# Recommender kernel: three placements moved in the last layers of the previous chunk (first transposes, second layer with its bias, Gelu)

## The chip, the cores and the metric

The kernel runs on one core of a Trainium2 chip. The metric is the device time in microseconds (us). TensorE (PE in the profile), VectorE (DVE), ScalarE (ACT), GpSimd (POOL) and the DMA queue of SyncE (SP) each work through their own instructions in order and meet at semaphores.

## The reference

2048 rows, each with 5 fields of 128 numbers (one of them attention over 50 history items), are expanded to 15 features of 128 (`TOTAL_DIM` = 1920). Then come two cross layers and a network of three layers:

```python
xc = dnn_in
for i in range(2):
    xc = dnn_in * (xc @ cross_K[i] + cross_bias[i]) + xc
h = gelu(_ln(xc @ w1 + b1, ln1g, ln1b), approximate=False)   # 1920 -> 512
h = gelu(_ln(h @ w2 + b2, ln2g, ln2b), approximate=False)    # 512 -> 256
logits = h @ w3 + b3
return sigmoid(logits)[:, 0]
```

The attention of one row scores each history item with a small network (`relu(x @ aw1 + ab1) @ aw2 + ab2`), takes the softmax and sums the items with these weights.

## The kernel before

The 16 tiles of 128 rows are cut into four chunks of four tiles (`T` = 4). After an opening, which does the attention of chunk 0, each chunk runs 30 steps `k` = 0 to 29 (15 output features of the first cross layer, then 15 of the second) and then the layer with `w1`. A step is three blocks of 15 matmuls on TensorE (`products(..., 0)`, `1`, `2`), each a third of the sum over the input features. Between the blocks TensorE's queue holds small work of two other kinds, put there by hand:

- The attention of the next chunk's tiles. `transposes(t, g, 0)` goes behind block 0 and `transposes(t, g, 1)` behind block 1, both for groups of ten history items; they write the PSUM tile `aps`, which a ScalarE copy (`copy_eT(0)`, `copy_eT(1)`) frees through `tp_free`. `hidden()` goes behind block 0 of the step after, `score()` behind its block 2. VectorE answers with `hidden_max`; in the step after that it does `softmax_max`, ScalarE does `exps` and `weigh`, and VectorE does `history` (a sum over the weighed items). `head_aim` stands on VectorE at the end of step 3 and of every sixth step after. Chunk 3 has no such work, because there is no chunk behind it.
- The last layers of the chunk ahead (`T and ...` in the code, in chunks 1 to 3 alone), at steps 2 to 9. For tile j: `fc_turn1(j)` transposes the normed `h1` of the tile into the fourth bank of `xps` (`FCB`); `fc_gelu1(j)` on ScalarE takes it out and frees the bank; `fc_w2(j)` multiplies by `w2` into the same bank; `fc_bias2(j)` on VectorE takes that out and frees the bank. `bank4_free` hands the bank round, so the order is turn1(j), gelu1(j), w2(j), bias2(j), turn1(j+1). `head_share` and `head_neg` of the attention use the same bank at steps 6 and 7. When all four tiles are through, `fc_stats`, `fc_sd` (a square root on ScalarE) and `fc_norms2` follow at step 6, `fc_turn2` at steps 7 and 8, `fc_w3` at step 9.

On ScalarE and VectorE each step also holds three `unit`s: `w_hi` rounds a weight block to the short form (`Wh`), `w_lo` subtracts it (`Wl`), for a block three ahead of the one at TensorE. Every `w_lo` waits for its `w_hi`. The order on VectorE in step k is: `x_sum`, `softmax_max`, first `w_lo`, `x_scale`, `fc_bias2`, `x_end`, `hidden_max`, `history`, second `w_lo`, `x_lo`, `times_target`, third `w_lo`, `head_aim` and `fc_stats`. On ScalarE it is: first `w_hi`, `exps` and `weigh`, `x_hi`, `copy_eT(0)`, second `w_hi`, `fc_gelu1`, `copy_eT(1)`, `fc_gelu2`, third `w_hi`, `fc_sd`.

Of the kernel before, what the change touches and what calls it, by code (L numbers as in the profile page):

```python
# [140 lines left out]
def build(nc, idx_d, table_d, cate_d, embT_d, rows_d, cols_d, mmw_d, aw1_d, bil_d, kx_d, w1_d, w2_d, out_d, ntiles):  # L141
    assert sum(TILES) == ntiles
    with ExitStack() as ctx:
# [92 lines left out]
        def h2(j):  # L236

            return h1[:, j, 0:H2]
# [91 lines left out]
        fvar_ready = sem("fvar_ready")  # L330
# [121 lines left out]
        def _(pe):  # L452
# [26 lines left out]
            def head_turn():  # L479
                pe.wait_ge(tgt_ready, 1).then_inc(tgt_ready, -1)  # L480
                pe.wait_ge(tp_free, 1).then_inc(tp_free, -1)
                nc.tensor.transpose(gps, tgt[:], ident[:]).then_inc(tp_ready, 1)
# [116 lines left out]
            def fc_turn1(j, bank=FCB):  # L599
                pe.wait_ge(h1n_ready, 1).then_inc(h1n_ready, -1)  # L600
                if bank == FCB:
                    pe.wait_ge(bank4_free, 1).then_inc(bank4_free, -1)
                for k in range(H1 // P):
                    last = nc.tensor.transpose(xps[:, bank, k * P:(k + 1) * P], h1[:, j, k * P:(k + 1) * P], ident[:])
                last.then_inc(fT_ready, 1)

            def fc_w2(j, bank=FCB):
                pe.wait_ge(g_ready, 1).then_inc(g_ready, -1)
                if bank == FCB:
                    pe.wait_ge(bank4_free, 1).then_inc(bank4_free, -1)  # L610
                for k in range(H1 // P):
                    last = mm(xps[:, bank, 0:H2], h1_T(j)[:, k, :], w2[:, k, :], start=(k == 0), stop=(k == H1 // P - 1))
                last.then_inc(fmm_ready, 1)
# [40 lines left out]
            def step(p):  # L654
                T, k = p.fc, p.k
                products(p.chunk, p.layer, p.n, 0)
                if T and 2 <= k < T + 2:
                    fc_turn1(k - 2)
                if p.open:
                    hidden()  # L660
                if p.pair is not None:
                    tail_bilinear()
                if p.grp:
                    transposes(*p.grp, 0)

                products(p.chunk, p.layer, p.n, 1)
                if p.grp:
                    transposes(*p.grp, 1)
                elif p.swing is not None:
                    head_turn()  # L670
                if T and k == T + 3:
                    fc_turn2(pairs(T)[0])
                if T > 2 and k == T + 4:
                    fc_turn2(pairs(T)[1])
                if T and k == T + 5:
                    fc_w3(T)

                products(p.chunk, p.layer, p.n, 2)
                if T and 2 <= k < T + 2:
                    fc_w2(k - 2)  # L680
                if p.share is not None:
                    head_share(p.share)
                if p.open:
                    score()
                if p.lift is not None:
                    tail_turn(p.lift)
# [13 lines left out]
            T = TILES[-1]  # L700
# [11 lines left out]
        def _(act):  # L712
# [36 lines left out]
            def copy_tT(t):  # L749
                act.wait_ge(tp_ready, 1).then_inc(tp_ready, -1)  # L750
                done(af(tT[:, t % 2, :], gps, ACT.Copy))
                act.sem_inc(tp_free, 1)
                act.sem_inc(tT_ready, 1)
# [81 lines left out]
            def fc_gelu1(j, bank=FCB):  # L835
                act.wait_ge(fT_ready, 1).then_inc(fT_ready, -1)
                for k in range(H1 // P):
                    last = af(h1_T(j)[:, k, :], xps[:, bank, k * P:(k + 1) * P], ACT.Gelu, scale=col("g1", k), bias=col("lb1", k))
                done(last)
                if bank == FCB:  # L840
                    act.sem_inc(bank4_free, 1)
                act.sem_inc(g_ready, 1)
# [55 lines left out]
            def step(p):  # L898
                c, k, T = p.chunk, p.k, p.fc

                if c and k == 0:
                    r_hi(c, FEATS - 1)
                if T and k == T + 6:
                    fc_exp(c - 1)
                if T and k == T + 7:
                    fc_out(c - 1)
                if p.pair is not None:
                    tail_copy(p.pair)
                unit(c, 3 * k)
                if p.fetch is not None:  # L910
                    head_fetch(p.fetch)
                if p.summed:
                    exps(*p.summed)
                    weigh(*p.summed)
                if p.n or p.layer:
                    x_hi(*((c, p.layer, p.n - 1) if p.n else (c, 0, FEATS - 1)))
                if p.gate is not None:
                    tail_gate()

                if p.grp:  # L920
                    copy_eT(0)
                unit(c, 3 * k + 1)
                if T and 2 <= k < T + 2:
                    fc_gelu1(k - 2)

                if p.grp:
                    copy_eT(1)
                elif p.swing is not None:
                    copy_tT(p.swing)
                if T and k == T + 3:  # L930
                    fc_gelu2(pairs(T)[0])
                if T > 2 and k == T + 4:
                    fc_gelu2(pairs(T)[1])
                unit(c, 3 * k + 2)
                if p.pair is not None:
                    tail_store(p.pair)
                if T and k in (1, T + 2):
                    fc_sd(T)
# [44 lines left out]
        def _(dve):  # L983
# [211 lines left out]
            def unit_out(c, b):  # L1195
                if c * STREAM + b + LOOK < TOTAL:
                    w_out()


            def fc_stats(j, x):  # L1200
                done(v.bn_stats(fstats[:], x))
                done(v.bn_aggr(fmv[:, j, :], fstats[:]))
# [13 lines left out]
            def fc_bias2(j, bank=FCB):  # L1216
                dve.wait_ge(fmm_ready, 1).then_inc(fmm_ready, -1)
                done(v.tensor_tensor(h2(j), xps[:, bank, 0:H2], row("b2"), ALU.add))
                if bank == FCB:
                    dve.sem_inc(bank4_free, 1)  # L1220
# [49 lines left out]
            def step(p):  # L1270
                c, k, T = p.chunk, p.k, p.fc
                prev = (c, p.layer, p.n - 1) if p.n else (c, 0, FEATS - 1) if p.layer else None

                if c and k == 0:
                    r_lo(c, FEATS - 1)
                if prev:
                    x_sum(*prev)
                if p.summed:
                    softmax_max(*p.summed)
                if T and k == 0:  # L1280
                    h1_rest(c - 1)
                unit(c, 3 * k)
                if prev:
                    x_scale(*prev)
                unit_out(c, 3 * k)
                if T and 3 <= k < T + 3:
                    fc_bias2(k - 3)
                if p.neg is not None:
                    head_neg(p.neg)
                if prev:  # L1290
                    x_end(*prev)
                if T and k == T + 2:
                    fc_stats(T - 1, h2(T - 1))
                    dve.sem_inc(fvar_ready, 1)
                if p.open:
                    hidden_max(p.open[0])
                if p.summed:
                    history(*p.summed)

                unit(c, 3 * k + 1)  # L1300
                if prev:
                    x_lo(*prev)
                unit_out(c, 3 * k + 1)
                if p.pair is not None:
                    tail_pairs()
                if p.grp:
                    times_target(p.grp[0])

                unit(c, 3 * k + 2)
                unit_out(c, 3 * k + 2)  # L1310
                if T and k == T + 6:
                    fc_probs(c - 1)
                if p.gate is not None:
                    tail_gate_apply(p.gate)
                if p.fold is not None:
                    tail_fold(p.fold)
                if p.aim is not None:
                    head_aim(p.aim)
                if T and k == 0:
                    for j in range(T):  # L1320
                        fc_stats(j, h1[:, j, :])
                    dve.sem_inc(fvar_ready, 1)
                if T and k == 1:
                    fc_norms1(T)
                if T and 3 <= k < T + 2:
                    fc_stats(k - 3, h2(k - 3))
                if T and k == T + 2:
                    fc_norms2(T)
# [115 lines left out]
```

## Time and profile before

| what | value |
|---|---|
| median of 3 runs | 2120.38 us (2118.11 to 2121.18) |
| span of the profiled execution | 2115.6 us |
| TensorE busy | 1937.3 us, 92% |
| VectorE busy | 1337.0 us, 63% |
| ScalarE busy | 904.3 us, 43% |
| mean granted TensorE clock | 0.941 |

The page cuts the span into 40 slices of 52.9 us. From the eighth on TensorE is busy for over nine tenths of each until near the end; the opening is the part where it is not. The timeline lists instructions in order of time; an idle stretch of the engine before an instruction stands behind it in brackets, with the line that ended it (`PEq L602` is the wait of TensorE's own queue on line 602).

### The profile page before, as it was taken

To read this page: it belongs to the slowest core of one execution; us is meant where nothing else is said; L and a number is where in the kernel's file an instruction comes from. 1 tells how busy PE (TensorE), PEld (TensorE's weight loads), DVE (VectorE), ACT (ScalarE), POOL (GpSimd) and SP (SyncE) were. 2 spreads that over 40 slices of the span, in tenths; PEclk is the share of its full clock that TensorE was granted. 3 is DMA by queue.
4 is the path that set the end of the run, shared out by engine and by line. 5 is a ranking of instruction groups with operands and counts; after the bars stand their busy time and mean duration, and the time that the engine had idled before them with its cause. 6 is when DMAs were issued, how large, how long until landed. Compare 5 with 4: busy or idle time off the path is not lost. (4 is left out here: it accounts for less than half of the span.)

```text
span 2115.6 us, 32889 instructions
## 1 busy us (share of the span) xinstructions
PE 1937.3 (92%) x9608; PEld 1518.8 (72%) x9608; DVE 1337.0 (63%) x2242; ACT 904.3 (43%) x1969; POOL 894.1 (42%) x854
## 2 busy tenths in 40 slices
PE   1765659999999999999999999999999999999997
PEld 1444437777777887777777886777777888888885
DVE  4564564767777755667777755666777664445543
ACT  1443443444444335654445235654445243322223
POOL 7777776555655512555555601555560000000000
PEclk7666568999999999999999999999999999999998
DMA  5111123334434452334434452334432442333330
GB/s 164 50 51 50 49 51 102 104 102 129 120 109 122 143 190 68 100 95 127 118 111 123 148 175 63 100 111 115 120 107 90 129 158 81 89 99 96 97 91 15
DMA packets 99679, 220.31 MB, mean 104 GB/s; under 512 B 21792, under 2 KB 27184, under 8 KB 99376
## 3 DMA queue, kind: packets, MB, share of 16 engines
q1 hardware_dynamic: 63072, 136.90, 21.5%
q0 software_dynamic: 27136, 55.63, 10.4%
q10 hardware_dynamic: 9296, 25.70, 3.2%
q8 instruction: 80, 1.31, 0.3%
q14 instruction: 95, 0.78, 0.1%
HBM read 205.29 MB, written 12.85 MB: 103 GB/s over the span
## 5 line engine op out<-in xcount | busy, mean ns | idle before, releaser
L415 POOL DMA_INDIRECT e<-in_item_table,idx_all x800 | 842.9, 1054 | 651.9 <-issue 303.8
L1148 DVE TENSOR_TENSOR Wl<-raw,Wh 128x640 fp32r<-128x640 f32 (+1 forms) x420 | 338.2, 805 | 286.6 <-DVEq L1147 283.0
L808 ACT ACTIVATE Wh<-raw 128x640 fp32r<-128x640 f32 (+1 forms) x420 | 301.8, 722 | 494.7 <-ACTq L807 493.7
L550 PE MATMUL xps<-X0h,Wh 128*128 128x512 f32 x900 | 364.7, 405 | 0.0
L550 PE MATMUL xps<-X1h,Wh 128*128 128x512 f32 x900 | 359.4, 399 | 0.0
L552 PE MATMUL xps<-X0h,Wl 128*128 128x512 f32 x900 | 352.1, 391 | 0.0
L551 PE MATMUL xps<-X0l,Wh 128*128 128x512 f32 x900 | 351.7, 391 | 0.0
L552 PE MATMUL xps<-X1h,Wl 128*128 128x512 f32 x900 | 351.0, 390 | 0.0
L551 PE MATMUL xps<-X1l,Wh 128*128 128x512 f32 x900 | 350.7, 390 | 0.0
L767 ACT ACTIVATE e<-e,pw 128x128 f32<-128x128 f32 x800 | 242.8, 388 | 15.4 <-ACTq L138 15.4
L552 PEld LDWEIGHTS xps<-X0h,Wl 128*128 128x128 f32 x900 | 169.4, 188 | 37.2
L552 PEld LDWEIGHTS xps<-X1h,Wl 128*128 128x128 f32 x900 | 168.9, 188 | 36.5
L550 PEld LDWEIGHTS xps<-X0h,Wh 128*128 128x128 f32 x900 | 169.8, 189 | 34.1 <-issue 2.1
L550 PEld LDWEIGHTS xps<-X1h,Wh 128*128 128x128 f32 x900 | 169.2, 188 | 33.6 <-issue 1.0
L551 PEld LDWEIGHTS xps<-X0l,Wh 128*128 128x128 f32 x900 | 170.1, 189 | 31.2
L551 PEld LDWEIGHTS xps<-X1l,Wh 128*128 128x128 f32 x900 | 169.4, 188 | 32.2
L1087 DVE TENSOR_REDUCE hist<-e 128x128 f32<-128x1280 f32 (+1 forms) x65 | 156.0, 2399 | 49.3 <-DVEq L1085 49.3
L736 ACT ACTIVATE eT<-aps 128x640 f32<-128x640 f32 x141 | 98.1, 696 | 166.6 <-ACTq L735 166.1
L1039 DVE TENSOR_TENSOR teT<-eT,tT 128x1280 f32<-128x1280 f32 x79 | 117.7, 1490 | 64.3 <-DVEq L1037 64.3
L492 PE MATMUL hps<-eT,A 128*64 128x512 f32 (+2 forms) x640 | 137.4, 509 | 19.7 <-PEq L486 19.6
L467 PE MATMUL aps<-ident,e 128*128 128x128 f32 x700 | 109.7, 290 | 37.9 <-issue 27.5
L496 PE MATMUL hps<-teT,A 128*64 128x512 f32 (+2 forms) x640 | 134.4, 499 | 0.0
(149 smaller groups left out, 2181.4 us busy)
## 6 DMA issues: line engine op xcount, KB each, us to landing
raw<-in_cross_K SPq DMA_DIRECT2D x360, 320.0 KB
raw<-in_w SPq DMA_DIRECT2D x60, 256.0 KB
e<-in_item_table,idx_all POOLq DMA_INDIRECT x800, 2.5
dnn_scratch<-dn ACTq DMA_DIRECT2D x12, 960.0 KB, 4.2
x1f<-dnn_scratch ACTq DMA_DIRECT2D x3, 2048.0 KB, 9.3
x1f<-dnn_scratch ACTq DMA_DIRECT2D x3, 1792.0 KB, 15.0
dn<-in_embT SPq DMA_DIRECT2D x1, 1024.0 KB, 5.3
img_scratch<-dn ACTq DMA_DIRECT2D x1, 1024.0 KB, 4.6
```

Of the source, the lines that this page charges most:

```text
L415: nc.gpsimd.indirect_dma_start(out=dst, out_offset=None, in_=table, in_offset=bass.IndirectOffsetOnAxis(ap=idx_all[:, t, s:s + 1], axis=0) ...
L467: last = nc.tensor.transpose(tps[:, s * P:(s + 1) * P], e_sub(t, g, u, s), ident[:])
L492: last = mm(hsum[u * HID:(u + 1) * HID, a:b], A12[:], eT[:, u, a:b], start=True, stop=False)
L496: last = mm(hsum[u * HID:(u + 1) * HID, a:b], A3[:], teT[:, u, a:b], start=False, stop=True)
L550: m0 = mm(out, wh, Xh[:, 0:T, k, :], start=(k == 0), stop=False)
L551: m1 = mm(out, wh, Xl[:, 0:T, k, :], start=False, stop=False)
L552: m2 = mm(out, wl, Xh[:, 0:T, k, :], start=False, stop=(k == FEATS - 1))
L767: last = af(x, x, ACT.Copy, scale=pw[:, g % 2, s:s + 1])
L808: af(Wh[:, split_slot(w), 0:n], raw[:, rs, 0:n], ACT.Copy).then_inc(hi_done, 1)
L1039: v.tensor_tensor(teT[:].rearrange("p u (s b) -> p (u s) b", b=P), eT[:].rearrange("p u (s b) -> p (u s) b", b=P), tT[:, par:par + 1, :].t ...
L1087: done(v.tensor_reduce(hist[:] if g else acc[:, par, :], x, AX.X, ALU.add))
L1148: v.tensor_tensor(Wl[:, rs, 0:n], raw[:, rs, 0:n], Wh[:, slot, 0:n].bitcast(F32), ALU.subtract).then_inc(lo_done, 1)
```

## The change

TensorE: `fc_turn1(k - 2)` moves from behind block 0 to behind block 1 and the second transposes of step k. `fc_w2` moves from behind block 2 of step k to behind block 0 of step k + 1. ScalarE: `fc_gelu1(k - 2)` moves from before to behind `copy_eT(1)`, still in step k and still before the third `w_hi`. VectorE: `fc_bias2(k - 3)`, and at step 6 the statistics of the last tile, move from behind the first `w_lo` to behind the second `w_lo` and `x_lo` of the same step. No instruction is added or taken away.

```diff
@@ tensor, step(p)
                 products(p.chunk, p.layer, p.n, 0)
-                if T and 2 <= k < T + 2:
-                    fc_turn1(k - 2)
+                if T and 3 <= k < T + 3:
+                    fc_w2(k - 3)
                 if p.open:
                     hidden()
...
                     head_turn()
+                if T and 2 <= k < T + 2:
+                    fc_turn1(k - 2)
                 if T and k == T + 3:
                     fc_turn2(pairs(T)[0])
...
                 products(p.chunk, p.layer, p.n, 2)
-                if T and 2 <= k < T + 2:
-                    fc_w2(k - 2)
@@ scalar, step(p)
                 unit(c, 3 * k + 1)
-                if T and 2 <= k < T + 2:
-                    fc_gelu1(k - 2)
-
                 if p.grp:
                     copy_eT(1)
                 elif p.swing is not None:
                     copy_tT(p.swing)
+                if T and 2 <= k < T + 2:
+                    fc_gelu1(k - 2)
@@ vector, step(p)
                 unit_out(c, 3 * k)
-                if T and 3 <= k < T + 3:
-                    fc_bias2(k - 3)
...
-                if T and k == T + 2:
-                    fc_stats(T - 1, h2(T - 1))
-                    dve.sem_inc(fvar_ready, 1)
...
                 unit_out(c, 3 * k + 1)
+                if T and 3 <= k < T + 3:
+                    fc_bias2(k - 3)
+                if T and k == T + 2:
+                    fc_stats(T - 1, h2(T - 1))
+                    dve.sem_inc(fvar_ready, 1)
```

## Rows read from the trace of the kernel before

**Rows 1.** The page: busy time of each engine, share of the span.

```profile
PE 1937.3 (92%) x9608; PEld 1518.8 (72%) x9608; DVE 1337.0 (63%) x2242; ACT 904.3 (43%) x1969; POOL 894.1 (42%) x854
```

**Rows 2.** Waits of TensorE: line <- released by: us in total, times, longest.

```profile
PE xps L604 <- PEq L602: 6.5, 2, 3.5
```

**Rows 3.** Timeline, TensorE, chunk 1: start, us, line, what, [idle before].

```profile
825.25 0.76 PE L467 MATMUL aps<-ident,e 128*128 128x128 f32 x5
829.27 0.71 PE L467 MATMUL aps<-ident,e 128*128 128x128 f32 x5
...
842.72 0.63 PE L604 MATMUL xps<-ident,dn 128*128 128x128 f32 x4 [3.04 <-PEq L602]
...
860.01 0.63 PE L604 MATMUL xps<-ident,dn 128*128 128x128 f32 x4
...
897.60 0.74 PE L467 MATMUL aps<-ident,e 128*128 128x128 f32 x5 [1.84 <-PEq L465]
```

**Rows 4.** Timeline, VectorE, chunk 1, from the end of step 3 to step 4.

```profile
825.48 0.82 DVE L1053 TENSOR_TENSOR hidT<-hps,negT 128x640 f32<-128x640 f32 x1 [3.39 <-DVEq L1052]
...
833.76 0.82 DVE L1148 TENSOR_TENSOR Wl<-raw,Wh 128x640 fp32r<-128x640 f32 x1
...
842.01 0.42 DVE L1218 TENSOR_TENSOR dn<-xps,rows 128x256 f32<-128x256 f32 x1
845.81 0.82 DVE L1053 TENSOR_TENSOR hidT<-hps,negT 128x640 f32<-128x640 f32 x1 [3.39 <-DVEq L1052]
...
847.02 2.46 DVE L1087 TENSOR_REDUCE hist<-e 128x128 f32<-128x1280 f32 x1 [0.26 <-DVEq L1085]
...
851.08 0.69 DVE L1189 TENSOR_TENSOR X1l<-x1f,X1h 128x512 fp32r<-128x512 f32 x1
...
854.09 0.82 DVE L1148 TENSOR_TENSOR Wl<-raw,Wh 128x640 fp32r<-128x640 f32 x1
```

**Rows 5.** Timeline, ScalarE, chunk 1, steps 3 to 5.

```profile
828.10 1.28 ACT L838 ACT_TABLE_LOAD   x1
...
831.32 0.71 ACT L736 ACTIVATE eT<-aps 128x640 f32<-128x640 f32 x1 [0.42 <-ACTq L735]
...
840.78 1.28 ACT L759 ACT_TABLE_LOAD   x1 [3.42 <-ACTq L757]
...
858.08 1.28 ACT L759 ACT_TABLE_LOAD   x1 [0.38 <-ACTq L757]
```

**Rows 6.** Timeline, VectorE, chunk 1, steps 6 and 7.

```profile
877.54 0.43 DVE L1201 BATCH_NORM_STATS2 tiny<-dn 128x6 f32<-128x256 f32 x1 [0.54 <-DVEq L1176]
...
886.81 0.18 DVE L1206 RECIPROCAL frstd<-fsd 128x4 f32<-128x4 f32 x1 [0.35 <-DVEq L1205]
...
896.38 2.37 DVE L1087 TENSOR_REDUCE hist<-e 128x128 f32<-128x1280 f32 x1 [2.12 <-DVEq L1085]
```

**Rows 7.** Timeline, ScalarE, chunk 1, steps 6 and 7.

```profile
884.92 1.28 ACT L833 ACT_TABLE_LOAD   x1
...
891.13 1.28 ACT L759 ACT_TABLE_LOAD   x1 [1.71 <-ACTq L757]
```

**Rows 8.** Timeline, TensorE, ScalarE and VectorE, chunk 3.

```profile
1811.83 0.60 PE L622 MATMUL xps<-ident,dn 128*128 128x128 f32 x4
...
1812.54 1.28 ACT L848 ACT_TABLE_LOAD   x1 [2.09 <-ACTq L845]
...
1765.06 0.74 ACT L808 ACTIVATE Wh<-raw 128x640 fp32r<-128x640 f32 x1 [1.29 <-ACTq L807]
...
1765.94 0.82 DVE L1148 TENSOR_TENSOR Wl<-raw,Wh 128x640 fp32r<-128x640 f32 x1 [2.00 <-DVEq L1147]
```

**Rows 9.** Timeline, chunk 2: TensorE at step 4, then VectorE's answer.

```profile
1315.54 1.09 PE L604 MATMUL xps<-ident,dn 128*128 128x128 f32 x4 [3.50 <-PEq L602]
...
1320.16 0.82 DVE L1053 TENSOR_TENSOR hidT<-hps,negT 128x640 f32<-128x640 f32 x1 [4.92 <-DVEq L1052]
```

**Rows 10.** Busy time by stretch (PE, PEld, DVE, ACT, POOL, PEclk, DMA share, GB/s).

```profile
1315.50:1319.00 3.50, 3.46 (x12) 1.52 (x14) 0.00 (x0) 3.35 (x11) 1.03 (x2) 0.54 0.13 37
```

## The prediction
> **What bounds the kernel now.** I read the page's busy times first: TensorE is busy 92% of the span, VectorE 63%, and the slices put most of TensorE's idle time into the opening [rows 1]. So from chunk 0 on an edit is worth what it adds to or takes from TensorE's idle time. Next come TensorE's waits: the only one in the chunks that names the moved code is line 602, the first transposes waiting for `bank4_free`, twice, 6.5 us in all, the longest 3.5 [rows 2]. Then the timelines, to see where. In chunk 1 the wait is 3.04 us at step 4 [rows 3], in chunk 2 it is 3.50 us at the same step [rows 9], and chunk 3 has none. The reader is to see why it is step 4: `fc_bias2`, which frees the bank, starts at 842.01 on VectorE, 0.71 us before the transposes at 842.72 [rows 3, 4]; it was late because `head_aim` lies between the third `w_lo` of step 3 (833.76) and the `softmax_max` that lets ScalarE's exponential begin (840.78), 7.02 us, where a step without `head_aim` takes 858.08 - 854.09 = 3.99 us [rows 4, 5]. At step 7 TensorE waits 1.84 us for `aps` (line 465), behind another chain [rows 3].
>
> **What the change removes.** The transposes no longer stand behind block 0, where `fc_bias2` was late. That gives back at most 3.04 + 3.50 us. In chunk 2 the wait also cost clock: the granted clock is 0.54 in the 3.50 us behind it [rows 10], that is, mostly the lower level (1.2 GHz), and from the transposes' start to `hidden_max` it is 4.62 us (1320.16 - 1315.54), against 845.81 - 842.72 = 3.09 us in chunk 1 [rows 3, 4, 9]: 1.53 us more. About 0.3 us of small waits at steps 3 and 5 may go too. The gain is at most 8.4 us. No instruction is added, and each moved piece still stands beside other small work, so I put nothing on TensorE's own work.
>
> **What the change adds: VectorE's side of the bank.** From step 3 on, the transposes of a tile wait for `fc_bias2` of the tile before, which now stands behind `hidden_max`, `history`, the second `w_lo` and `x_lo` of the same step. I count from the start of `hidden_max`, H, which comes as TensorE ends `hidden`. `x_lo` starts at H + 5.27 (851.08 - 845.81) [rows 4], `fc_bias2` about 0.6 later (the length of `x_lo`, 0.69, less its overlap), and the transposes 0.71 after its start: H + 6.6. TensorE reaches them after the second transposes of the attention: those start at 829.27, 3.79 after H (825.48), and last about 0.5, so at H + 4.25 [rows 3, 4]. The new wait is 2.35 us at steps 4 and 5. At step 3 `history` handles a first group and has no accumulation behind it, some 0.6 less: 1.75 us. What queues behind the waiting transposes is block 2, so all of TensorE.
>
> **What the change adds: a loop through three engines.** `fc_gelu1` on ScalarE now waits for transposes that are late in the step, and behind it in ScalarE's queue stands the third `w_hi`; VectorE's third `w_lo` waits for that, and behind `w_lo` stand `head_aim` and the next step's `softmax_max`. S is the start of the transposes.
> - S to ScalarE's table load for Gelu: 0.71 (1812.54 - 1811.83, a like pair in chunk 3) [rows 8].
> - Table load, Gelu and the link behind it, to the next instruction: 831.32 - 828.10 = 3.22 [rows 5]. So the third `w_hi` starts at S + 3.93.
> - `w_hi` to `w_lo`: 0.88 (1765.94 - 1765.06) [rows 8]. S + 4.81.
> - `w_lo` to the exponential's table load: 3.99, with `head_aim` 7.02 (above).
> - From there to `history`, which needs the weighed items: 896.38 - 891.13 = 5.25 [rows 6, 7].
> - `history` to `x_lo` 4.06 (851.08 - 847.02), to `fc_bias2` 0.6, to the next transposes 0.71: 5.37 [rows 3, 4].
>
> The sum is 4.81 + 3.99 + 5.25 + 5.37 = 19.4 us per step, and 22.45 us from step 3 to step 4 with `head_aim`. Step 4 to step 5 took 860.01 - 842.72 = 17.29 us before [rows 3]. So the loop is longer than TensorE's step, and each step runs at the loop's time. TensorE is then the waiter, though its work is the same.
>
> **The sum for chunk 1**, as the start of block 2 of each step (before: H + 4.25; after: S + 0.35, since the four transposes add that to the ones beside them):
> - Step 3: H was 825.48; without the transposes ahead of it 0.65 less, 824.8. S = 824.8 + 6.0 = 830.8, block 2 at 831.2 against 829.7: 1.4 us late.
> - Step 4: S = 830.8 + 22.45 = 853.3, block 2 at 853.6 against 850.06: 3.6 us late (gaps of about 5.5 us in place of 3.04; part of them before the second transposes, since `copy_eT(0)`, which frees `aps`, is behind `weigh`).
> - Step 5: S = 853.3 + 19.4 = 872.7, block 2 at 873.1 against 845.81 + 17.29 + 4.25 = 867.35: 5.7 us late.
> - Steps 6 and 7: the exponential's load is at 872.7 + 4.81 + 3.99 = 881.5, `history` at 886.8, `fc_bias2` 4.66 later at 891.4, and with the last tile's statistics (which took 0.43 and a little more [rows 6]) ScalarE's square root loads at about 892.9. It was at 884.92 [rows 7], so 8.0 us late. What hangs on it is as before: reciprocal 1.89 later, then 4.32 to the exponential's load at 891.13, then 6.47 to the second transposes at 897.60 [rows 3, 6, 7]. They come at about 905.6: 8.0 us late, in place of a wait of 1.84 some 4.3.
>
> `head_share` at step 6 needs the bank as well: `fc_bias2` at 891.4 frees it by 892.1, and TensorE is there at about 892.1, so nothing is added. Behind step 7 the same waits follow as before. **Chunk 2** is the same with 0.46 us more of old wait and 1.53 us of old clock loss in its time: 8.0 - 2.0 = 6.0 us. **Chunk 3** has no `history`, no exponential and no late `x_lo`: the transposes come a whole block later and so does the bank; 0, at most 0.5 us. Sum without the clock: 14.0 us.
>
> **The clock.** A gap of 3.50 us was followed by a low clock [rows 9, 10], and one of 3.04 us was not: there `hidden_max` follows the transposes at the ordinary 3.09 us [rows 3, 4]. The new gaps of about 5.5 us at step 4 (in two pieces) and 4.3 us at step 7, in both chunks, are four such places. One lapse cost 1.53 us [rows 9], at step 4 nearly all of it added because the path by H is 19.2 us, close to the loop. I take two of the four, 3.0 us, with 0 and 6.1 as the bounds. The Trainium skill ("TensorE: Matmul & The Clock Gate", Part 1: The HAM clock gate) says that an idle array falls back to half rate and only activity releases it, which speaks against this change; the chunk 2 gap agrees, at 0.54. By that rule all four places would lapse, and the time would be 2140.5 us.
>
> **The rivals.**
> - The gain that the moved lines offer: TensorE finds the bank free in all steps. 2120.4 - 8.4 = 2112.0 us. For it: the transposes come a block and more later in the step. Against: `fc_bias2` moves by more, 851.7 against 842.01 at step 4 (9.7 us), and the transposes by about 7.3 (from 839.68, where the wait began, to 850.06 less the 3.04 us of wait). It decides if `history` were short; it is 2.46 us [rows 4].
> - VectorE's delay alone, without the loop (if `w_hi` did not have to wait for Gelu): each step takes the path by H, 19.2 us, step 4 too, and block 2 is late by 1.4, 0.3 and 2.2 us; the square root then follows `fc_bias2` of step 6 and step 7 is 4.2 us late. Chunk 1 +4.2, chunk 2 +2.2: 2126.8 us. Against: `unit(c, 3 * k + 2)` stands behind `fc_gelu1` in ScalarE's queue.
> - All four lapses and waits carried into steps 8 and 9: 14.0 + 6.1 + 2 to 6 us, 2143 to 2147 us. For it: step 7 already waits before the change [rows 3], so a lapse in its block 2 could meet the next copy late. Against: VectorE and ScalarE are held by the same TensorE and come later with it.
> - No difference that shows: the new waits equal the old in size. It needs new waits of 5 us a chunk; the least that I find is the second rival's.
>
> **How the numbers follow.** The profiled span, 2115.6 us, is 4.8 us under the median, which I take as constant. Forecast: 14.0 + 3.0 = 17.0 us, a span of 2132.6, a median of 2137.4 us. Chances: the forecast (2131 to 2141) 0.56; VectorE's delay alone (2124.6 to 2131) 0.15; all lapses 0.12; no difference 0.08; the gain 0.09. About 0.2% (4.2 us) is what a measurement of this kernel tells from no change. Slower by more: 0.83; within: 0.08; faster: 0.09. The range leaves out the gain, no difference and the top of the third rival: 2124 to 2145 us.
>
> **What would show it.** In the profile after: line 602 as TensorE's largest wait of the chunks, at steps 3, 4 and 5 of chunks 1 and 2 with about 1.8, 3.4 and 2.4 us; a wait on line 465 at step 4 of about 2 us and at step 7 of about 4; the third `w_hi` right behind Gelu and the third `w_lo` 0.9 us behind that; chunk 3 unchanged. I am wrong on the loop if step 4 to step 5 takes under 19 us from transposes to transposes, and wrong on the direction if line 602 no longer appears.

## The result, and the profile after

| | before | after |
|---|---|---|
| median | 2120.41 us (2118.11 to 2121.18) | 2140.45 us (2139.80 to 2141.72) |
| span of the profiled execution | 2115.6 us | 2138.9 us |
| TensorE busy | 1937.3 us | 1941.0 us |
| mean granted TensorE clock | 0.941 | 0.937 |

The ratio of after to before is 1.0089, with a 95% interval of 1.0077 to 1.0101: the changed kernel is 20.0 us slower by the medians, 23.3 us by the two profiled spans. I had forecast 17.0 us. The first two figures differ because the profiled execution of before was a quick one: in the changed kernel a run's time is 1.8 us over its span, and so I estimate that before's profiled execution took 2117.4 us, 3.0 under its median. Where those 3 us lie is open, since before has one profile only.

First TensorE's waits in the changed kernel (line <- released by: us in total, times, longest), to be held against [rows 2]. `L467` is the attention's transposes waiting for `aps`, `L604` the first transposes of the last layers waiting for the bank.

```profile
PE aps L467 <- PEq L465: 17.4, 11, 3.9
PE xps L604 <- PEq L602: 13.8, 6, 3.3
```

The reader is to see the count: two bank waits have become six. The timeline of TensorE in chunk 1 shows where; the number in brackets is the wait.

```profile
831.60 0.63 PE L604 MATMUL xps<-ident,dn 128*128 128x128 f32 x4 [1.52 <-PEq L602]
...
849.94 0.74 PE L467 MATMUL aps<-ident,e 128*128 128x128 f32 x5 [1.58 <-PEq L465]
853.99 1.08 PE L604 MATMUL xps<-ident,dn 128*128 128x128 f32 x4 [3.31 <-PEq L602]
...
875.40 1.09 PE L604 MATMUL xps<-ident,dn 128*128 128x128 f32 x4 [2.08 <-PEq L602]
...
909.71 1.30 PE L467 MATMUL aps<-ident,e 128*128 128x128 f32 x5 [3.89 <-PEq L465]
```

These are steps 3, 4, 4, 5 and 7; chunk 2 has the same five (1.51, 1.80, 3.31, 2.08 and 3.91 us), chunk 3 none. Where [rows 3] had 0.63 us for four transposes and 0.74 us for five, three of these groups are drawn out (1.08, 1.09 and 1.30 us): the clock is low there, as the windows further down show.

One stretch serves from here on as the measure of every kernel: from the second attention transposes of step 1 to those of step 9, in chunks 1 and 2. The columns are length, then busy time of PE, PEld, DVE, ACT and POOL, granted clock, DMA share, GB/s. The kernel before:

```profile
797.70:929.40 131.70, 125.10 (x663) 96.69 (x664) 82.72 (x143) 81.17 (x161) 57.53 (x53) 1.00 0.31 88
1270.05:1403.40 133.35, 126.54 (x664) 97.27 (x664) 82.70 (x143) 81.16 (x161) 55.49 (x53) 0.99 0.31 87
```

The changed kernel:

```profile
798.40:942.30 143.90, 130.39 (x664) 100.86 (x665) 82.86 (x143) 80.92 (x161) 55.75 (x53) 0.95 0.28 80
1282.80:1427.20 144.40, 130.33 (x663) 100.85 (x664) 83.01 (x143) 80.91 (x161) 55.03 (x53) 0.95 0.28 80
```

The two stretches have grown by 12.2 and 11.05 us, together 23.25 us, which is the whole difference of the spans (3 us more than that of the medians). Length less TensorE's busy time is its idle time: 6.6 + 6.8 us before, 13.5 + 14.1 us after, so 14.2 us are new waits. The other 9.1 us are busy time: the same matmuls (664, one record more or less) took 125.10 and 126.54 us, and now 130.39 and 130.33 us. VectorE and ScalarE worked as long as before.

The low clock by stretch: the end of the wait of step 4, then the time after the waits of step 4, step 5 and step 7 of chunk 1. The clock is the column before the DMA share:

```profile
850.00:854.00 4.00, 0.69 (x6) 0.48 (x6) 3.19 (x5) 1.44 (x2) 1.64 (x2) 0.68 0.00 0
854.00:858.00 4.00, 4.00 (x12) 3.32 (x13) 1.49 (x1) 2.79 (x5) 3.09 (x4) 0.50 0.32 70
875.40:879.00 3.60, 3.60 (x11) 3.04 (x12) 1.49 (x1) 2.39 (x5) 2.99 (x3) 0.53 0.21 44
909.70:913.20 3.50, 3.50 (x14) 3.16 (x15) 3.00 (x5) 2.42 (x3) 1.13 (x2) 0.54 0.08 19
```

The last three are nearly all at the lower level (1.2 GHz). At step 4 the clock has fallen before the wait is over (0.68), and stays low for 4 us of work more. The loop through the three engines can be read off between step 3 and step 4 (ScalarE, VectorE; VectorE's line numbers are one lower than before):

```profile
832.34 1.28 ACT L838 ACT_TABLE_LOAD   x1 [1.34 <-ACTq L836]
...
835.55 0.74 ACT L808 ACTIVATE Wh<-raw 128x640 fp32r<-128x640 f32 x1 [0.42 <-ACTq L807]
...
843.48 1.28 ACT L759 ACT_TABLE_LOAD   x1 [5.61 <-ACTq L757]
```

```profile
836.44 0.83 DVE L1147 TENSOR_TENSOR Wl<-raw,Wh 128x640 fp32r<-128x640 f32 x1 [3.29 <-DVEq L1146]
...
848.72 2.35 DVE L1086 TENSOR_REDUCE hist<-e 128x128 f32<-128x1280 f32 x1 [2.53 <-DVEq L1084]
...
853.27 0.42 DVE L1217 TENSOR_TENSOR dn<-xps,rows 128x256 f32<-128x256 f32 x1
```

From the transposes at 831.60: Gelu's table load 0.74 later, third `w_hi` at + 3.95, third `w_lo` at + 4.84 after 3.29 us of waiting for it, the exponential's load 7.04 behind that with `head_aim` between, `history` 5.24 later after 2.53 us of waiting for `weigh`, `fc_bias2` 4.55 later, the next transposes 0.72 later at 853.99.

### The profile page after: what moved, and what is told of

Same layout as the page of the kernel before. It is cut to its first block and busy times, and to the rows that moved or that the text cites. A ratio compares the mean times of both kernels' runs of the same rounds, so it can differ in the third digit from the quotient of the medians.

```text
span 2138.9 us, 32889 instructions
## 1 busy us (share of the span) xinstructions
PE 1941.0 (91%) x9608; PEld 1522.7 (71%) x9608; DVE 1336.4 (62%) x2242; ACT 903.6 (42%) x1969; POOL 891.4 (42%) x854
## 5 line engine op out<-in xcount | busy, mean ns | idle before, releaser
L467 PE MATMUL aps<-ident,e 128*128 128x128 f32 x700 | 110.6, 292 | 46.4 <-issue 29.0
L467 PEld LDWEIGHTS aps<-ident,e 128*128 128x128 f32 x700 | 85.1, 149 | 71.3 <-issue 63.5
```

The lines of the kernel that those rows point to most:

```text
L467: last = nc.tensor.transpose(tps[:, s * P:(s + 1) * P], e_sub(t, g, u, s), ident[:])
```

## The experiments

In the table, "waits" is TensorE's idle time in the two stretches, "busy" its busy time there. The rows e1 to e9 are the experiments in the order of the sections below.

| kernel | median, us | ratio to before (95%) | stretches, us | waits, us | busy, us |
|---|---|---|---|---|---|
| before | 2120.4 | | 265.05 | 13.4 | 251.6 |
| after | 2140.5 | 1.0089 (1.0077 to 1.0101) | 288.3 | 27.6 | 260.7 |
| e1_bias_early | 2120.5 | 0.9994 (0.9985 to 1.0003) | 267.6 | 12.1 | 255.5 |
| e2_gelu_late | 2134.5 | 1.0062 (1.0048 to 1.0076) | 281.7 | 22.1 | 259.6 |
| e3_both | 2109.1 | 0.9944 (0.9930 to 0.9957) | 255.3 | 6.3 | 249.0 |
| e4_aim_moved | 2133.4 | 1.0055 (1.0042 to 1.0069) | 266.6 | 12.4 | 254.2 |
| e5_filled | 2134.1 | 1.0059 (1.0045 to 1.0073) | 279.3 | 7.6 | 271.7 (46 matmuls more in each) |
| e6_bias_first | 2122.4 | 1.0005 (0.9996 to 1.0014) | 267.7 | 13.9 | 253.8 |
| e7_after_again | 2139.5 | one run | 288.2 | 27.7 | 260.5 |
| e8_norms_late | 2107.2 | 0.9938 (0.9924 to 0.9951) | 253.2 | 4.1 | 249.1 |
| e9_both_again | 2109.0 | 0.9944 (0.9931 to 0.9958) | 255.6 | 6.4 | 249.2 |

The kernel before had medians of 2120.5 to 2121.5 us beside these. Of the stretches each row is one profile. Two kernels were profiled twice, and their stretches agree to 0.1 us (288.3 and 288.2) and 0.3 us (255.3 and 255.6). Ahead of chunk 1 all but e4 run the same code, yet they reach the first row of the stretch anywhere from 796.9 to 802.4 us: single spans differ by that without any cause in the change.

### VectorE's move undone

```diff
                 unit_out(c, 3 * k)
+                if T and 3 <= k < T + 3:
+                    fc_bias2(k - 3)
                 if p.neg is not None:
                     head_neg(p.neg)
                 if prev:
                     x_end(*prev)
+                if T and k == T + 2:
+                    fc_stats(T - 1, h2(T - 1))
+                    dve.sem_inc(fvar_ready, 1)
...
                 unit_out(c, 3 * k + 1)
-                if T and 3 <= k < T + 3:
-                    fc_bias2(k - 3)
-                if T and k == T + 2:
-                    fc_stats(T - 1, h2(T - 1))
-                    dve.sem_inc(fvar_ready, 1)
```

> The changed kernel with fc_bias2 and the last tile's statistics put back behind VectorE's first w_lo. My theory: VectorE then waits there for fc_w2, which ends over 2 us before hidden, so hidden_max is not late; the bank is free when TensorE comes to the transposes, line 602 disappears from its waits, and the loop through Gelu, softmax_max and history no longer has a way back to the transposes. What stays is a wait of 1.5 to 2 us on aps (line 465) at step 4 and the old 1.84 us at step 7. Against before: - 3.04 - 3.50 - 1.53 - 0.3 + 2 x 1.9 = -4.6 us, 2115.8 us. Rival: ScalarE's order (Gelu ahead of the third w_hi) costs the time by itself; then it stays over 2130 us with waits on aps at each step.

Measured: 2120.53 us, the time of the kernel before. TensorE has no wait on the bank left in chunks 1 and 2; what is left at steps 4 and 7 of chunk 1 are waits for `aps`:

```profile
852.91 0.96 PE L467 MATMUL aps<-ident,e 128*128 128x128 f32 x5 [2.26 <-PEq L465]
...
903.34 0.74 PE L467 MATMUL aps<-ident,e 128*128 128x128 f32 x5 [2.37 <-PEq L465]
```

The theory is right on the bank and the rival is out: 20.7 of the stretches' 23.25 us go with this one edit. The gain that I expected on top did not come, for two reasons. The wait at step 4 is 2.26 us, not 1.9, and step 7's grew from 1.84 to 2.37 us; and behind these waits the clock is low (0.55 and 0.67 in the 3.5 us that follow, chunk 1), so that busy time is 3.9 us above that of before.

### Gelu behind the third `w_hi`

```diff
                 elif p.swing is not None:
                     copy_tT(p.swing)
-                if T and 2 <= k < T + 2:
-                    fc_gelu1(k - 2)
...
                 unit(c, 3 * k + 2)
+                if T and 2 <= k < T + 2:
+                    fc_gelu1(k - 2)
```

> The changed kernel with fc_gelu1 put behind ScalarE's third w_hi; everything else of the change stays. My theory: VectorE's third w_lo no longer waits for Gelu, so only the path hidden_max, history, w_lo, x_lo, fc_bias2 is left: waits on line 602 of about 1.8, 2.4 and 2.4 us at steps 3, 4 and 5, step 4 no longer the longest, chunk 1 +4.2 us and chunk 2 +2.2 us, 2126.8 us, up to 2131 where the clock lapses. Rival: the late fc_bias2 is the whole cause and the loop adds nothing; then it stays at 2138 us or more.

Measured: 2134.51 us. TensorE in chunk 1, steps 3, 4, 5 and 7:

```profile
831.59 0.63 PE L604 MATMUL xps<-ident,dn 128*128 128x128 f32 x4 [1.50 <-PEq L602]
...
851.12 0.63 PE L604 MATMUL xps<-ident,dn 128*128 128x128 f32 x4 [2.23 <-PEq L602]
...
872.12 0.63 PE L604 MATMUL xps<-ident,dn 128*128 128x128 f32 x4 [2.08 <-PEq L602]
...
906.43 0.74 PE L467 MATMUL aps<-ident,e 128*128 128x128 f32 x5 [3.89 <-PEq L465]
```

The waits on the bank are the ones that the path through `hidden_max` and `history` gives, and step 4 is no longer apart: 2.23 us in place of 1.58 + 3.31. From step 3 to step 4 it is 19.53 us between the transposes (851.12 - 831.59), where the changed kernel has 22.39. So the loop is real, and it is worth 5.5 us of waiting in the two stretches (27.6 - 22.1). But the time is 3.5 us above the top of what I expected, since the clock falls behind three waits of each chunk here too (in chunk 1 0.70, 0.63 and 0.60 in the 3.5 us from each of the last three rows); the busy time is 8 us above that of before.

### Both edits

The edits of the two kernels above together; TensorE's new order stays.

```diff
@@ scalar, step(p)
-                if T and 2 <= k < T + 2:
-                    fc_gelu1(k - 2)
...
                 unit(c, 3 * k + 2)
+                if T and 2 <= k < T + 2:
+                    fc_gelu1(k - 2)
@@ vector, step(p)
                 unit_out(c, 3 * k)
+                if T and 3 <= k < T + 3:
+                    fc_bias2(k - 3)
...
+                if T and k == T + 2:
+                    fc_stats(T - 1, h2(T - 1))
+                    dve.sem_inc(fvar_ready, 1)
...
                 unit_out(c, 3 * k + 1)
-                if T and 3 <= k < T + 3:
-                    fc_bias2(k - 3)
-                if T and k == T + 2:
-                    fc_stats(T - 1, h2(T - 1))
-                    dve.sem_inc(fvar_ready, 1)
```

> The changed kernel with both edits: fc_bias2 behind VectorE's first w_lo, fc_gelu1 behind ScalarE's third w_hi. TensorE's new order stays. My theory: no wait on line 602, at most 0.7 us on aps at step 4, step 7 as before: 2112 to 2114 us, faster than before. Rival: TensorE's new order itself costs (more changes between kinds of matmul, later tiles at steps 6 and 7); then it is at 2120 us or above.

Measured: 2109.07 us, 12.3 us under before, and 2108.95 us when run again (below), 11.6 under. The two stretches:

```profile
797.00:924.80 127.80, 124.58 (x663) 96.59 (x664) 82.58 (x143) 81.13 (x161) 58.11 (x53) 1.00 0.31 90
1265.40:1392.90 127.50, 124.44 (x663) 96.56 (x664) 82.51 (x143) 81.13 (x161) 57.12 (x53) 1.00 0.30 91
```

The granted clock is 1.00 in both, and no wait stands at step 4 at all. The wait at step 7 is 1.61 us. So TensorE's new order costs nothing that shows, once the other two engines' queues fit it, and the rival is out. This kernel and the one with VectorE's move undone differ in the place of Gelu alone, and that is worth 12.3 us of the stretches (267.6 - 255.3). How much of the gain over before belongs to TensorE's order and how much to Gelu's place is not shown: no run has the old order with Gelu moved. It beat the expected 2112 us by 3 us. Step 7's wait fell a little too, and the busy time of chunk 1 is 124.58 us where before had 125.10, both at a clock of 1.00; that the transposes now run beside others of their kind may be why, but no run tests it.

### `head_aim` moved, in the kernel before

```diff
-            fetch, aim, swing = s - 6, s - 4, s - 1
+            fetch, aim, swing = s - 6, s - 2, s - 1
```

> The kernel before with head_aim of the tiles of later chunks two steps later (at step 5 and every sixth after, in place of step 3): no transposes wait for the bank at step 6. My theory: head_aim is what made fc_bias2 late at step 4, so line 602 disappears from the waits, worth 3.04 + 3.50 + 1.53 us; but softmax_max of step 6 is then about 3.0 us late, history 2.7 us, and the wait on aps at step 7 grows from 1.84 to about 4.5 us. Sum 5.3 - 8.1 = -2.8 us, 2117.6 us, or 2120.6 us where the clock lapses at step 7. Rival: something else makes fc_bias2 late at step 4 (ScalarE's w_hi, the score); then the wait on line 602 stays at 3 us and the time is 2123 us or more.

Measured: 2133.43 us, a miss by 13 us. In the part that it was made for it did what I said: chunk 1 has no wait on the bank, chunk 2 one of 0.66 us, and the wait at step 7 has taken its place, with a low clock behind it (0.50 in 3.5 us). TensorE, steps 1 and 7 of chunk 1:

```profile
810.93 0.74 PE L467 MATMUL aps<-ident,e 128*128 128x128 f32 x5 [1.02 <-PEq L465]
...
910.63 1.30 PE L467 MATMUL aps<-ident,e 128*128 128x128 f32 x5 [4.73 <-PEq L465]
```

The stretches are 1.6 us longer than before. The larger part of the loss, 13.2 us, is there when chunk 1 begins (810.93 against 797.74), 8.5 us later than in the latest of the other kernels: the edit also moved `head_aim` of the other tiles of chunks 1 to 3, in the opening and in chunk 0. What it did there was not taken apart.

### TensorE kept at work in the waits of the changed kernel

```diff
+            FILL = {3: (0, 6), 4: (6, 12), 5: (0, 8), 7: (14, 0)}
+            def fill(p, at):
+                ...
+                for i in range(FILL[p.k][at]):
+                    mm(out, Wh[:, split_slot(w), 0:P], X0h[:, 0:TILES[c], 0, :], start=True, stop=True)
...
                 products(p.chunk, p.layer, p.n, 1)
+                fill(p, 0)
                 if p.grp:
                     transposes(*p.grp, 1)
                 elif p.swing is not None:
                     head_turn()
+                fill(p, 1)
```

TensorE's wait for the next output feature's bank (`bank_free`) moves ahead of these matmuls with them.

> The changed kernel with extra matmuls on TensorE (fp32r, 512 columns, 0.23 us apart, into the bank of the next output feature, which is not yet in use) in front of the waits of chunks 1 and 2: 6 ahead of the first transposes at step 3, 6 ahead of the second attention transposes and 12 ahead of the first transposes at step 4, 8 at step 5, 14 ahead of the second attention transposes at step 7. They are work for nothing, 46 matmuls or 10.5 us a chunk, shorter than each wait that they stand in. My theory: some 9.5 us of the change's cost is the low clock behind the waits; with TensorE kept at work it stays high, and the time falls from 2140 to about 2131 us (2129 to 2133), with no stretch of low clock in chunks 1 and 2. Rival: the time is in the waits alone and the low clock is absorbed by them; then the filled kernel stays at 2140 us or goes above, since it has more work.

Measured: 2134.11 us, 1.1 us above the expected range and 6.3 us faster than the changed kernel (5.4 against its run beside this one), with 92 matmuls more.

```profile
799.80:939.50 139.70, 135.92 (x710) 104.81 (x711) 83.03 (x143) 80.70 (x161) 56.44 (x53) 1.00 0.29 83
1280.10:1419.70 139.60, 135.77 (x710) 104.88 (x710) 82.95 (x143) 80.69 (x161) 55.73 (x53) 1.00 0.29 83
```

The clock column says 1.00. The stretches are 9.0 us shorter than those of the changed kernel (279.3 against 288.3), close to the 9.1 us that its busy time had gained over before. So that some 9 us of the loss come with the low clock is shown, not only read, and the rival is out. The match is in part chance: before has 1.5 us of low clock in its own stretches, so the changed kernel has about 10.6 (an estimate: 260.7 less twice the 125.1 of before's chunk 1), and the filled kernel is some 15.8 us over a kernel before without it. Removing 10.6 us of low clock gave 9.0 us, and the waits took up the rest. The median fell by less than the stretches. From transposes to transposes, steps 4 and 5, at the high clock:

```profile
855.50 0.63 PE L617 MATMUL xps<-ident,dn 128*128 128x128 f32 x4 [0.59 <-PEq L615]
...
874.96 0.63 PE L617 MATMUL xps<-ident,dn 128*128 128x128 f32 x4 [0.31 <-PEq L615]
```

19.46 us, against the 19.4 us of the prediction's sum. This figure doesn't tell the loop from the path through `hidden_max`, which took 19.53 us without the loop (above): from step 4 to step 5 the two are equally long. What shows the loop is step 3 to step 4, where `head_aim` lies in it.

### `fc_bias2` ahead of `softmax_max`, in the kernel before

```diff
                 if prev:
                     x_sum(*prev)
+                if T and 3 <= k < T + 3:
+                    fc_bias2(k - 3)
                 if p.summed:
                     softmax_max(*p.summed)
...
-                if T and 3 <= k < T + 3:
-                    fc_bias2(k - 3)
```

> The kernel before with fc_bias2 put ahead of softmax_max on VectorE, behind x_sum; nothing else. My theory: the bank is then free 2.6 us earlier, the wait on line 602 at step 4 falls from 3.04 and 3.50 us to about 0.4 and 0.9 us, the lapse of the clock in chunk 2 goes (1.53 us), exponential and step 7 come 0.5 us later: -3.04 - 3.50 - 1.53 + 1.3 + 0.5 to 1 = -6 us, 2115 us. Rival: the wait at step 4 was slack that the later steps need, and it turns up again at step 7; then 2120 to 2121 us.

Measured: 2122.37 us, no difference; the rival was right. The wait at step 4 fell to 0.40 us as computed, and the one at step 7 grew from 1.84 to 3.83 us, with the clock low behind it (0.54 in 3.5 us):

```profile
840.55 0.63 PE L604 MATMUL xps<-ident,dn 128*128 128x128 f32 x4 [0.40 <-PEq L602]
...
899.29 1.30 PE L467 MATMUL aps<-ident,e 128*128 128x128 f32 x5 [3.83 <-PEq L465]
```

ScalarE's table loads for the exponential at steps 4, 5 and 6 tell why:

```profile
842.02 1.28 ACT L759 ACT_TABLE_LOAD   x1 [4.19 <-ACTq L757]
...
859.82 1.28 ACT L759 ACT_TABLE_LOAD   x1 [2.96 <-ACTq L757]
...
877.62 1.28 ACT L759 ACT_TABLE_LOAD   x1 [2.96 <-ACTq L757]
```

They are 17.80 us apart. ScalarE and VectorE hand each other a round (exponential, `weigh`, first copy, Gelu, second copy, `times_target`, third `w_lo`, `fc_bias2`, `softmax_max`) that is longer here than TensorE's step of 17.3 us in the kernel before. The edit itself made it so. Its last part starts with this row, the third `w_lo` of step 4:

```profile
855.06 0.82 DVE L1148 TENSOR_TENSOR Wl<-raw,Wh 128x640 fp32r<-128x640 f32 x1
```

From there to the exponential's load it is 4.76 us, where [rows 4, 5] have 3.99: `fc_bias2` now stands in between. Without these 0.77 us the round would be 17.03 us, still only 0.26 under the step (an estimate). So the 3 us by which `head_aim` puts the two engines behind at step 3 are not made up; they come out at the next long wait. In the kernel before, TensorE's wait at step 4 held it back by as much, and the loads are 17.30 us apart [rows 5]. In the kernel with both edits Gelu is out of that round. Its loads of steps 4 and 5:

```profile
838.37 1.28 ACT L759 ACT_TABLE_LOAD   x1 [3.65 <-ACTq L757]
...
853.65 1.28 ACT L759 ACT_TABLE_LOAD   x1 [1.82 <-ACTq L757]
```

They are 15.28 us apart, 2 us under the step, so the 3 us are made up within two steps. That this is why its wait at step 7 stayed short is read from these rows; in the old order of TensorE no run moved Gelu alone.

### The changed kernel once more

> The changed kernel once more, for a second profile. My theory: the waits of chunks 1 and 2 are the same to 0.1 us and the stretches of low clock stand behind the same waits (steps 4, 5 and 7 of both chunks). If where the clock falls is a matter of chance, other waits are followed by it, and the waits of step 5 (2.08 us) in one chunk or the other are not.

Measured: 2139.54 us. Transposes of steps 4 and 5 in chunk 1:

```profile
852.59 1.08 PE L604 MATMUL xps<-ident,dn 128*128 128x128 f32 x4 [3.30 <-PEq L602]
...
873.98 1.09 PE L604 MATMUL xps<-ident,dn 128*128 128x128 f32 x4 [2.08 <-PEq L602]
```

The waits agree to 0.11 us, and the granted clock in the stretches behind steps 4, 5 and 7 is 0.50, 0.53 and 0.54 in both chunks; the first profile has the same to 0.01. In these two executions, and in both chunks of each, where the low clock fell was no matter of chance.

### Both edits, and `fc_norms2` a step later

```diff
                 if T and k == T + 2:
                     fc_stats(T - 1, h2(T - 1))
                     dve.sem_inc(fvar_ready, 1)
+                if T and k == T + 3:
+                    fc_norms2(T)
...
-                if T and k == T + 2:
-                    fc_norms2(T)
```

> The kernel with both edits (fc_bias2 behind the first w_lo, fc_gelu1 behind the third w_hi), and fc_norms2 moved from the end of step 6 to step 7, behind x_end. What it tells: whether the wait on aps at step 7 comes from VectorE's softmax_max standing behind fc_norms2. My theory: 2.3 us of it leave the chain to the exponential, so the wait of 1.61 us goes to zero in chunks 1 and 2 and the time falls by 3.2 us against the kernel with both edits. Rival: weigh itself (3 us behind the exponential's table load) sets that wait; then it stays over 1 us and the time is the same.

> The kernel with both edits once more, beside the one with fc_norms2 moved. My theory: 2109 us again (2107 to 2111), no stretch of low clock in chunks 1 and 2.

Measured: 2107.22 us with `fc_norms2` moved, 2108.95 us without. The wait at step 7 is 0.49 us, where the one beside it has 1.63 us in chunk 1 and 1.65 us in chunk 2:

```profile
896.77 0.74 PE L467 MATMUL aps<-ident,e 128*128 128x128 f32 x5 [0.49 <-PEq L465]
```

So `softmax_max` behind `fc_norms2` was most of that wait, not all: half a microsecond stays, where I had expected none, and the rival (over 1 us) is out. Against before the ratios are 0.9938 (0.9924 to 0.9951) and 0.9944 (0.9931 to 0.9958), so the difference between the two is not told by the times; the waits tell it. Both are faster than before and after.

## Why the prediction was right, and where it was off

- **What the change removes.** Right: no bank wait stands behind block 0 any longer. It was no gain, because other waits took its place at the same step (1.58 + 3.31 us for 3.04).
- **VectorE's side of the bank.** Right in place and nearly in size: waits on line 602 at steps 3, 4 and 5 of chunks 1 and 2 and nowhere else; 1.52 us at step 3 for 1.75, 2.08 at step 5 for 2.35, and 2.23 at step 4 with the loop out of the way. Putting `fc_bias2` back removed them all.
- **The loop.** Right: 22.39 us from the transposes of step 3 to those of step 4 (853.99 - 831.60) for 22.45, and its parts as listed above to within 0.11 us each; without the loop it was 19.53. From step 4 to step 5 it was 21.41 us for 19.4, since TensorE's own path to `hidden_max` ran at the low clock and became the longer one; at the high clock it was 19.46, which both paths give. One price in it bears on a page: the Trainium skill ("ScalarE: Activation LUTs", What ACT_TABLE_LOAD costs) puts a switch of tables at some 2.7 us, the load and a drain behind it. Here the load is 1.28 us and the Gelu begins 1.29 us after the load's start in both kernels, so no drain stands between them; the measurement decides, and the term from the trace held.
- **Step 7.** The wait on `aps` is 3.89 us for the 4.3 forecast, the second transposes there are 11.4 us late for 8.0 (909.71 - 897.60, less the 0.7 us by which this execution came later into the chunk). The surplus is low clock at steps 4 and 5: in the filled kernel, at the high clock, step 4 to step 5 takes 1.95 us less and step 5 to step 7 1.55 us less (32.76 for 34.31), 3.5 us together. The prediction's own sum gives a wait of 4.1 us (1.84 + 8.0 - 5.7), not the 4.3 it states.
- **Steps without cost.** `head_share` waits for nothing, and chunk 3 has no wait on the bank, as computed.
- **The waits together.** The sum of 14.0 us is called "without the clock", but the 1.53 us of old clock loss are already taken off in it. The waits that it forecasts are 15.5 us (8.0 + 7.5); measured are 14.2, and about 15.8 over before at the high clock (the filled kernel).
- **The clock: the term that was mis-sized.** I took two places of 1.53 us, 3.0 us, with 6.1 as the upper bound; it was 9.1 us on top of the 1.5 us that before had, 10.6 us for six places, 1.8 us each. The total came within the stated range because the range was wide and the waits came out 1.3 us under. Two things were wrong. I counted only gaps above 3.5 us as places, from two gaps of the kernel before (3.50 with a lapse, 3.04 without), and took half of those; the 2.08 us at step 5 were enough. And at step 4 the low clock lasted longer than behind the gap of [rows 9, 10]: it began within the wait, and 4.0 us of work after it ran at 0.50. The four places that I named did all lapse, and two more came at step 5, behind 2.08 us each. That all four would lapse is what the prediction drew from the rule of the Trainium skill ("TensorE: Matmul & The Clock Gate", Part 1: The HAM clock gate). The 2140.5 us that it gave for this case is the measured median only by luck, since six places lapsed and not four.
- **From span to median.** The profiled execution of before lies 4.8 us under its median, that of after 1.55 us under. The 4.8 us are not constant: by the estimate above 1.8 of them are, and 3.0 belong to the one execution that was profiled. By the spans I was 6.3 us too low, by the medians 3.0. That the median came out so near is in part luck.
- **The rivals.** The gain that the moved lines offered was there, but needed both other queues to change: 12.3 us with both edits, more than the 8.4 us that I took as the most. VectorE's delay alone (2126.8 us) came out at 2134.5 us: the waits in the stretches were 8.7 us over before for 7.9 (the 6.4 with the old clock loss put back), and the clock added 8.0. Of the third rival the four lapses came, but nothing was carried into steps 8 and 9: the wait at step 9 is 1.12 us in chunk 1 and 1.47 in chunk 2, as before the change (1.16 and 1.47).
- **The signs.** Line 602 waited at the steps named, 1.52, 3.31 and 2.08 us for 1.8, 3.4 and 2.4. It was not TensorE's largest wait of the chunks: line 465 was, with 3.89 us at step 7 and more in all.

## What to carry to other kernels

When a piece of work is moved in one engine's queue, follow what now stands behind it in the others': here one Gelu ahead of a rounding that another engine waits for, and one bias behind a reduction, closed a loop longer than the step. Write the loop's length beside the step's; a wait on the busiest engine may be only the place where a delay of the others comes out, and removing it alone moves it. And count what follows a wait: here two microseconds idle at step 5 cost some 1.5 us more in clock.

## What the runs showed of the hardware that I had not expected

- The clock fell behind short gaps: 2.08 us at step 5 was followed by a granted clock of 0.53 over 3.6 us, in both chunks and in both profiles of the changed kernel, and 2.26 us in the first experiment by 0.55 over 3.5 us. A single wait of 1.84 us or less was not followed by it in chunks 1 and 2 of the kernels shown, but neither was the 3.04 us of [rows 3], whose neighbours in the queue are the same as those of the 3.50 us in [rows 9]. What decides besides the length is open.
- Work for nothing made the kernel faster: 92 matmuls more in the waits, 6.3 us less, at a granted clock of 1.00 through both stretches.
- The low clock came back in the same places: two executions of the changed kernel had it behind the same six waits of chunks 1 and 2.
